# Graph network kernel: products for the node table and the message table over 128 rows of TensorE's array, with zeros in the added rows

## The reference

```python
h = jnp.maximum(_layernorm(x, axis=-1), 0.0)
x = x + L0(h)   # softplus MLP on [h[dst], edge_attr_64] @ W1 + b1, summed by dst
h = jnp.maximum(_layernorm(x, axis=-1), 0.0)
x = x + L1(h)   # Ht = einsum('tmh,nh->tnm', A, h); msg = Ht[type, src]; summed by dst; GRU
h = jnp.maximum(_layernorm(x, axis=-1), 0.0)
x = x + L2(h)   # pair interaction weighted by a basis of 8, tanh, summed by dst
h = jnp.maximum(_layernorm(x, axis=-1), 0.0)
x = x + L3(h)   # two mean-aggregating convolutions
```

## Time and profile before

| What | Value |
|---|---|
| Three runs | 10609.83, 10613.77, 10619.3 us (median 10613.77) |
| Profiled execution, its own time | 10609.71 us |
| Its span in the trace | 10608.1 us |
| Mean granted clock over the span | 0.685 |
| Busy: PE / DVE / ACT / POOL | 56% / 41% / 23% / 65% |

### The profile page before, as it was taken

One profiled execution on the slowest core, in us unless ns is written; L12 is line 12 of the kernel. 1 busy time (PEld: TensorE's weight loads), 2 busy tenths in 40 slices (PEclk: granted clock), 3 DMA queues, 4 the chain that ended last, 5 costly groups with the idle time before them and its releaser, 6 DMA issues.

```text
span 10608.1 us, 144590 instructions
## 1 busy us (share of the span) xinstructions
PE 5928.7 (56%) x31865; PEld 3642.0 (34%) x32026; DVE 4356.3 (41%) x11981; ACT 2422.2 (23%) x4618; POOL 6911.9 (65%) x7936
## 2 busy tenths in 40 slices
PE   6999997344444447888888882343333322222222
PEld 4777773222222223333333331232223211111111
DVE  5888884222322224666666662111111111111111
ACT  4999992000000002333333330000000000000000
POOL 2333330577777776766666666777777767777777
PEclk9999995555555558999999995555555555555555
DMA  3333332111111112222222221111111111111111
GB/s 96 97 97 97 97 96 79 48 29 30 29 30 29 30 30 48 57 56 56 56 56 56 56 51 23 28 28 28 28 28 28 28 24 28 28 28 28 28 28 27
DMA packets 503888, 488.54 MB, mean 46 GB/s; under 512 B 245340, under 2 KB 299425, under 8 KB 503777
## 3 DMA queue, kind: packets, MB, share of 16 engines
q0 software_dynamic: 220480, 235.58, 11.8%
q1 hardware_dynamic: 283360, 252.43, 8.2%
HBM read 427.04 MB, written 61.15 MB: 46 GB/s over the span
## 4 chain that ended last, share of the span: by engine, by line
POOL 43%; PE 25%; issue 19%; DVE 8%; DVEq 2%; POOLq 1%; ACT 1%; DMA 0%; another core or an unknown queue 0%; ACTq 0%; SPq 0%
POOL mov L668 43%; PE ps L1524 5%; PE ps L1413 4%; PE ps L1387 3%; PE ps L1420 3%; DVE scr L937 3%; PE ps L1516 2%; PE ps L1449 2%; PE ps L1543 1%; DVE sel L927 1%; PE ps L1411 1%; PE ps L1534 1%; DVE acc L946 1%; PE ps L1427 1%; PE ps L1428 0%
## 5 line engine op out<-in xcount | busy, mean ns | idle before, releaser
L1387 PE MATMUL ps<-outs,mov 128*64 128x64 f32 x9984 | 1371.0, 319 | 4210.3 <-DMA mov<-tab_q,idx 1613.2
L1387 PEld LDWEIGHTS ps<-outs,mov 128*64 128x64 f32 x9984 | 1158.7, 222 | 4538.9 <-issue 4538.9
L837 DVE TENSOR_TENSOR acc<-acc,ps 64x64 f32 (+1 forms) x1664 | 353.6, 213 | 4432.5 <-PE ps L1387 4430.3
L668 POOL DMA_INDIRECT outs<-tab_u,idx x1664 | 1595.7, 959 | 735.8 <-issue 472.5
L668 POOL DMA_INDIRECT mov<-tab_msg,idx x1664 | 1575.4, 947 | 759.6 <-issue 492.2
L668 POOL DMA_INDIRECT mov<-tab_h,idx x1664 | 1570.2, 944 | 576.2 <-issue 506.5
L668 POOL DMA_INDIRECT mov<-tab_q,idx x1664 | 1570.2, 944 | 543.8 <-issue 506.5
L937 DVE TENSOR_TENSOR scr<-ps,scr 128x512 f32<-128x512 f32 x1664 | 1050.8, 682 | 266.7 <-PE ps L1516 184.2
L1524 PE MATMUL ps<-scr,w_bas 128*64 128x512 f32 x3328 | 899.9, 619 | 0.0
L631 POOL TENSOR_TENSOR scr<-outs 128x128 f32<-128x128 f32 x416 | 191.8, 461 | 834.9 <-DVE outs L847 834.0
L847 DVE TENSOR_TENSOR outs<-rel,iota_w 128x256 f32<-128x256 f32 x1664 | 705.4, 424 | 43.3 <-issue 30.2
(11 more groups left out here) (215 smaller groups left out, 8602.6 us busy)
## 6 DMA issues: line engine op xcount, KB each, us to landing
mov<-in_dst_row SPq DMA_DIRECT2D x832, 128.0 KB, 2.7
mov<-in_ea_T SPq DMA_DIRECT2D x416, 128.0 KB, 2.5
tab_msg<-outs SPq DMA_DIRECT2D x104, 256.0 KB, 2.0
mov<-tab_msg,idx POOLq DMA_INDIRECT x1664
outs<-tab_u,idx POOLq DMA_INDIRECT x1664
mov<-tab_h,idx POOLq DMA_INDIRECT x1664
mov<-tab_q,idx POOLq DMA_INDIRECT x1664
win<-tab_g SPq DMA_DIRECT2D x416, 32.0 KB, 2.4
```

Of the source, the lines that this page charges most:

```text
L668: nc.gpsimd.indirect_dma_start(out=gat(e, u)[:, k, :], out_offset=None, in_=table, in_offset=bass.IndirectOffsetOnAxis(ap=idx[:, u, k:k + ...
L837: nc.vector.tensor_tensor(into, into, bank(banks[u % len(banks)])[0:rows, 0:W], ALU.add) \
L1387: last = mm(bank(banks[u % len(banks)])[0:width, 0:W], values(u)[:, k, :], sel(e, u)[:, k, :], start=k == 0, stop=k == TL - 1)
```

## The change

The tiles hT, w_l0n and w_typ get 128 rows. POOL fills rows 64 to 127 of each with zeros, before the row of ones of hT is set, so there are three more constants. The products of T0 and T1 use all 128 rows; the other products that read hT are cut to the 65 rows they had. The load of L0_b1 into row 64 of w_l0n is taken out of LOADS and issued after them, behind a wait for all constants.

```diff
-        hT = sb("hT", [D + 1, 2, GN])
+        hT = sb("hT", [P128, 2, GN])
...
-        w_l0n = sb("w_l0n", [D + 1, H])
+        w_l0n = sb("w_l0n", [P128, H])
...
-        w_typ = sb("w_typ", [D, NT * D])
+        w_typ = sb("w_typ", [P128, NT * D])
...
-            (w_l0n[0:D, :], t["L0_W1"][0:D, :]), (w_l0n[D:D + 1, :], t["L0_b1"]), (w_l0m[:, :], t["L0_W2"]),
+            (w_l0n[0:D, :], t["L0_W1"][0:D, :]), (w_l0m[:, :], t["L0_W2"]),
...
-        ALL_LOADED = 16 * len(LOADS)
-        N_CONSTS = 24
+        ALL_LOADED = 16 * (len(LOADS) + 1)
+        N_CONSTS = 27
...
             for dst, src in LOADS:
                 sp.dma_start(dst, src).then_inc(loaded, 16)
+            sp.wait_ge(consts, N_CONSTS)
+            sp.dma_start(w_l0n[D:D + 1, :], t["L0_b1"]).then_inc(loaded, 16)
...
-            for tile_, value in ((ones[:, :], 1.0), (ones_b[:, :], 1.0), (eps_c[:, :], EPS), (hT[D:D + 1, :, :], 1.0),
+            for tile_, value in ((ones[:, :], 1.0), (ones_b[:, :], 1.0), (eps_c[:, :], EPS),
+                                 (hT[D:P128, :, :], 0.0), (w_typ[D:P128, :], 0.0), (w_l0n[D:P128, :], 0.0), (hT[D:D + 1, :, :], 1.0),
...
-                    mm(bank(2 + k), hT[0:D, s, k * P128:(k + 1) * P128], w_typ[:, :], start=True, stop=True) \
+                    mm(bank(2 + k), hT[:, s, k * P128:(k + 1) * P128], w_typ[:, :], start=True, stop=True) \
...
-                        last = mm(out_, hT[:, 0, cols], w_hh[:, :], start=False, stop=True)
+                        last = mm(out_, hT[0:D + 1, 0, cols], w_hh[:, :], start=False, stop=True)
```

More of the change, by code:

```diff
@@ L410, in build_gnn @@
         LOADS = [
-            (w_l0n[0:D, :], t["L0_W1"][0:D, :]), (w_l0n[D:D + 1, :], t["L0_b1"]), (w_l0m[:, :], t["L0_W2"]),
+            (w_l0n[0:D, :], t["L0_W1"][0:D, :]), (w_l0m[:, :], t["L0_W2"]),
             (w_l0o[:, 0:D], t["L0_W3"]), (b_l0o[:, 0:D], t["L0_b3"].to_broadcast([P128, D])),
-            (w_typ[:, :], t["A_T"]), *((tab[SG * SN:NP, :], t["x"][SG * SN:NP, :]) for tab in (tab_u, tab_v, tab_h, tab_q)),
+            (w_typ[0:D, :], t["A_T"]), *((tab[SG * SN:NP, :], t["x"][SG * SN:NP, :]) for tab in (tab_u, tab_v, tab_h, tab_q)),
             (w_hh[0:D, 0:2 * D], t["w_hh_T"][:, 0:2 * D]), (w_hh[0:D, 3 * D:4 * D], t["w_hh_T"][:, 2 * D:3 * D]),
@@ L1481, in pp1 @@
                     wait_flow(pe, f, "lifted", turn0, g, 1)
-                    mm(bank(3)[0:D, 0:SN], w_pp1[:, :], hT[:, 1, 0:SN], start=True, stop=True) \
+                    mm(bank(3)[0:D, 0:SN], w_pp1[:, :], hT[0:D + 1, 1, 0:SN], start=True, stop=True) \
                         .then_inc(f.sems["formed"], 1)
@@ L1575, in conv1 @@
                         mm(bank(1)[:, cols], own_sum[0:D, cols], w_c1l[:, :], start=True, stop=True)
-                        last = mm(bank(1)[:, SN + k * P128:SN + (k + 1) * P128], hT[:, 0, cols], w_c1r[:, :],
+                        last = mm(bank(1)[:, SN + k * P128:SN + (k + 1) * P128], hT[0:D + 1, 0, cols], w_c1r[:, :],
                                   start=True, stop=True)
```

## The result

The changed kernel takes 10500.69 us (median of 4 runs, 10497.85 to 10503.56) against 10614.38 us before in the same comparison: a ratio of 0.9893, 95% interval 0.9876 to 0.991, 113.7 us less. The profiled execution's span is 10496.2 us against 10608.1, 111.9 less.

The account below looks back on a forecast made before the run. T1 was taken as bound by PE at its lower clock, the later edge stages as paced by POOL's gathers. Terms -92.6 + 1.9 + 7 - 7 + 1.8 = -88.9 gave 10520.8, median 10525; range 10500 to 10580.

Parts of the forecast that it names:

- (c): T1, message table: PE falls to the lower clock in half of 12 pauses, 1.2 us each: +7 us, bounds 0 to 24.
- (d): T0, node table: upper clock level reached only in part: -7 us; -22.0 at best, 0 if it stays low.
- the best case: Whole kernel: T1 and T0 rise fully, no falls in pauses, fills paid: -111 us, 10503.
- What bounds T1: Message table loop: PE at its lower clock level, busy 205.79 of 212.00 us, 16.47 us a pair.
- T0 is at the lower level although its clock row reads 1.00: Node table: transposes take 1.03 us as in T1, against 0.59 at the upper level, so the clock record is wrong.
- (a): T1 at the upper clock level: a pair takes 9.35 instead of 16.47 us, 13 pairs: -92.6 us.
- (b): Start of T1: PE must first rise, losing 1.9 to 5.6 us; taken as +1.9.
- (e): Starting chain: three more memsets on POOL delay DVE's first instruction: +1.8 us.
- (f): Loads at the start: L0_b1's load moved behind a wait for POOL's constants: cost 0, with 6 us of cover.
- No rise: Rival, 13%: something other than rows keeps T1 low; only the fills' 1.8 us is paid, median 10616.
- The moved load lands late: Rival, 2%, slower: L0_b1's load lands at 66, 13 us behind the fold; 10629 if T1 doesn't rise.
- Stores become the bound: Rival, 8%: T1's store landing doubles to 4.0 us, T1 saves 66, about 62 in all: 10552.

Follow-up runs that it names:

- rows_80: Changed kernel with T0's and T1's products over 80 rows instead of 128: ratio 1.0006 to the kernel before, in a set where every kernel was slower.
- ones_in_w_typ: Changed kernel with w_typ's added rows filled with 1.0 instead of 0.0: 10493.66 us, ratio 0.9892 to the kernel before.
- rows_96: Changed kernel with T0's and T1's products over 96 rows instead of 128: 10495.12 us, ratio 0.9893 to the kernel before.
- t0_long_pause: Changed kernel with an unused ACT copy of 2048 columns ahead of each staging in T0: T0 takes 100 us instead of 52 (slower set, total not used).
- fills_only: Changed kernel with its tiles, fills and moved load, but T0's and T1's products cut to 65 and 64 rows: 10610.83 us, ratio 1.0003 to the kernel before.
- the two single stages: Changed kernel with 128-row products in one stage only: T1 alone 10517.96 us (0.9914 to the kernel before), T0 alone 10586.17 us (0.9979).
- longer_pause: Changed kernel with an unused ACT copy of 3328 columns ahead of each staging in T1: T1 takes 171 us instead of 118 (slower set, total not used).

## Why the prediction held, point by point

The gain was forecast at 88.9 us and came out at 113.7. The mechanism is the one forecast; the sizes of two terms, (c) and (d), are not, and both erred to the same side. So the measured 10500.69 is below even the best case of 10503 and within the range of 10500 to 10580 by 0.7 us only, which is luck. Point by point:

- *What bounds T1*: PE at its lower level. Right: the loop went from 16.47 to 9.08 us a pair. Nearly all of it is the clock: in rows_80, at the lower level, a pair takes 16.16 us (products from 1718.42, the next from 1734.58), so only 0.31 of the 7.39 came without a rise.
- *T0 is at the lower level although its clock row reads 1.00*: right. Its transposes went from 1.03 to 0.60, its records from 0.214 apart to 0.121, so there was a level to gain there.
- *(a) 92.6 saved*: right in mechanism, a little small. Records are 0.439 apart, not 0.455: the row I used has two records between products of other lines, not a run of 16. What makes those two longer isn't shown. 16.47 - 9.08 = 7.39 a pair, 96.1 for 13.
- *(b) the rise costs 1.9*: the first pair took 8.98 instead of 7.02, 1.96. That is near the middle of what other traces of the same loop show: its first pair lost 0.9 in ones_in_w_typ and 2.2 in rows_96.
- *(c) falls in the pauses, +7*: wrong size; none occurred. The pause is 2.06 us, and T1 kept its level through 12 of 12; even 3.8 us broke it in 3 of 12, and 4.7 us in 12 of 12. Half of the pauses was too many, drawn from one pause of 3.25 us with sparse work around it. (The bound of 24 is 12 x 0.48 x 4 = 23.)
- *(d) T0, -7*: wrong size, and the largest miss. The stretch from T0's first product to its last went from 74.8 to 51.9 us, -22.9, the best case of my bounds. I held the products' small share against it; T0 kept the level in every pair once it had risen; in t0_long_pause pauses of 4.4 to 5.3 us undid it.
- *(e) +1.8*: DVE's first instruction moved from 14.99 to 16.83, 1.84; fills_only shows it alone.
- *(f), the moved load, 0*: the fold starts 1.84 later than the earlier trace rows, which is (e); PE's first product starts earlier, 43.68 against 44.59.
- *No rise*: no; the changed kernel rises with zeros in the added rows, and ones in w_typ's took the same time. (This is the rival that the prediction means by "the third rival's time"; it stands second in the list.)
- *The moved load lands late*: no. It is the last of the loads to land, and its landing released PE's first product, 0.9 us earlier than before and 9.2 us ahead of the fold at 52.93:

```profile
43.68 0.47 PE L1339 MATMUL ps<-tT 64*64 64x64 f32 x2 [43.68 <-DMA w_l0n<-in_L_b]
```

- *Stores become the bound*: no. Landing stayed at 2.0 us with DMA's share at 0.60, and no wait of DVE for a store shows in T1.

With the measured sizes: -96.1 + 1.96 - 22.9 + 1.84 = -115.2, and the first gather did start 115.2 us earlier (1806.40 against 1921.64). The span is 111.9 shorter. Of the 3.3 us given back, 2.4 are in the interaction stage, where PE once fell to its lower level after it had waited for DVE; the timeline of the changed kernel:

```profile
4254.89 0.39 PE L1519 MATMUL ps<-bas,pair 128*128 128x512 bf16 x1 [1.59 <-DVE scr L940]
...
4255.81 1.88 PE L1527 MATMUL ps<-scr,w_bas 128*64 128x512 f32 x4
...
4258.58 1.45 PE L1527 MATMUL ps<-scr,w_bas 128*64 128x512 f32 x4
...
4260.98 1.08 PE L1527 MATMUL ps<-scr,w_bas 128*64 128x512 f32 x4
```

The stage took 2352.29 us from its first gather to the next stage's, 2349.84 before, 2351.8 in rows_96 and 2349.2 in ones_in_w_typ, whose T0 and T1 are as fast. Counted from the stage's first gather, the gathers of the changed kernel run about 0.6 us behind those of before up to this fall and 3.6 behind after it, and some 1.3 come back at the end, where only the kernel before has the fall of the earlier trace rows. rows_96 has the fall near 4255 too, ones_in_w_typ doesn't. So I take this as that stage's own variation and not as the change's doing. That is argued from these four traces, not tested.

The step that decided the time, that rows in use and not the time in use kept PE low, was inferred from T1 and the edge MLP differing in rows among other things. fills_only, the two single stages and the row counts show it: the same products in the same loop, with only the row count changed. The rule of the Trainium skill (TensorE: Matmul & The Clock Gate, Part 1), that sustained activity releases the clock, agrees with this case only with enough rows: at 64, 72 and 80 of them over 200 us of nearly full PE released nothing (1067, 1062 and 1061 ns a record), and at 96 and 128 the first pair did (610 and 608 ns).

## What to carry to other kernels

Where a stretch is bound by TensorE, read the length of its records, and not only the busy share: a loop at 97% busy can run at half clock for all its life. If its products contract over 64 to 80 rows, fill them up with zeros to 96 or 128: for these f32 products the added rows cost nothing at either level, and each such stage ran at twice the clock from the end of its first pair on. Check then what is right behind (copies, stores, the pause between groups), and keep the pause short: it is the next thing to gain, and long pauses lose the level, here 0 of 12 at 2.06 us, 3 of 12 at 3.8 and 12 of 12 at 4.7. These counts are T1's; in the interaction stage, with little work around it, a wait of 1.59 us was followed by a fall.

## What was not expected of the hardware

- T1 with 80 rows stays at the lower level for 207 us of nearly full PE, and with 96 rows it rises within the first pair. The added rows of hT are zeros all the while; so rows in use count, also where they hold nothing.
- T0 keeps the upper level although its products take only 1.94 of each pair's 4.03 us.
- DVE's cast and POOL's memset slow each other when they run together: 1.03 to 1.63 us and 0.52 to 1.29 us.
- In longer_pause the level isn't yet lost at the end of the pause of 4.7 us: the four transposes there still take 0.60 us, and the products right behind them begin slow.
